# State space scan with C broadcast by DMA and ScalarE, D term on TensorE and its tail on GpSimd; one merged mask in differential attention

## What is computed

```python
def _L2_attn_ref(x, ...):            # differential attention, 32 maps of width 8
    att = einsum('bhtd,bhsd->bhts', q, k) * (1.0 / sqrt(hd))
    att = softmax(where(causal, att, -inf), axis=-1)
    att = att.reshape(B, H, 2, T, T)
    att = att[:, :, 0] - lambda_full * att[:, :, 1]
    out = einsum('bhts,bhsd->bhtd', att, v)
    out = out * rsqrt(mean(out * out) + EPS) * gamma * (1.0 - LAMBDA_INIT)
    return out.reshape(B, T, C) @ w_proj

def _L3_attn_ref(x, ...):            # state space, 512 channels, 16 states
    x_in, z = split(x @ W_in)
    xc = silu(conv4(x_in))                      # 4 taps
    dt, Bm, Cm = split(xc @ W_x, [16, 16, 16])
    delta = softplus(dt @ W_dt + b_dt)
    for t in frames:
        h = h * exp(delta * -exp(A_log)) + (delta * xc) * Bm
        y = sum_over_states(h * Cm)
    y = (y + xc * D) * silu(z)
    hh = x + y @ W_out
    return (hh - mean(hh)) * rsqrt(var(hh) + 1e-5) * gamma + beta
# the tower: h = h + _L2_attn_ref(_layernorm(h), ...) ; later h = h + _L3_attn_ref(_layernorm(h), ...)
```

## Time and profile before

| | us |
|---|---|
| median of 3 runs (lowest to highest) | 4446.45 (4444.82 to 4450.03) |
| the profiled execution | 4441.89, its span 4440.2 |
| differential attention, its loop over utterances | 1494 to 2078 |
| state space, scope | 2740 to 3915 |

### The profile page before, as it was taken

How to read it: one execution, slowest core, us unless ns; L and a number is a source line. 1 busy time by engine, 2 the same in 40 slices (tenths; PEclk the granted TensorE clock), 3 DMA queues, 4 the chain that set the end, 5 groups by cost and what they waited for, 6 DMA issues and landing times. The chain is left out here.

```text
span 4440.2 us, 70612 instructions
## 1 busy us (share of the span) xinstructions
PE 3466.3 (78%) x23831; PEld 2262.3 (51%) x23832; DVE 2241.4 (50%) x4136; ACT 1150.8 (26%) x2267; POOL 1169.3 (26%) x904
## 2 busy tenths in 40 slices
PE   7589954669975999998149961678887788759999
PEld 3367732347753677776139951333333333245777
DVE  0444455224443355554523333478988889941343
ACT  2221110111211122122224420344433444303222
POOL 0112211011211233332530026344444444510121
PEclk9798866778888999998579985789888888869999
DMA  1000002630002000001521112000000000000000
GB/s 43 11 1 0 0 2 43 99 42 0 0 11 83 1 0 0 0 0 33 148 52 47 47 47 56 28 21 25 25 21 21 21 24 25 14 22 0 7 10 11
DMA packets 241137, 115.45 MB, mean 26 GB/s; under 512 B 174305, under 2 KB 225315, under 8 KB 241040
## 3 DMA queue, kind: packets, MB, share of 16 engines
q1 hardware_dynamic: 221136, 98.04, 8.9%
q0 software_dynamic: 18432, 12.40, 1.2%
q10 hardware_dynamic: 1472, 3.85, 0.3%
HBM read 79.03 MB, written 35.02 MB: 26 GB/s over the span
## 5 line engine op out<-in xcount | busy, mean ns | idle before, releaser
L2107 POOL TENSOR_TENSOR ssm_dBx<-ssm_du,ssm_b_wide 128x1488 f32<-128x1488 f32 x128 | 430.1, 3363 | 325.9 <-DVE ssm_state L2364 324.5
L2364 DVE TENSOR_TENSOR_SCAN ssm_state<-ssm_dA,ssm_dBx 128x372 f32<-128x372 f32 x512 | 434.2, 909 | 34.8 <-ACT ssm_dA L2175 19.5
L2254 PE MATMUL ssm_y<-ssm_hC,top_ident 128*128 128x512 f32 (+1 forms) x768 | 430.6, 706 | 9.0 <-DVE ssm_hC L2369 7.5
L2175 ACT ACTIVATE ssm_dA<-ssm_delta,ssm_decay 128x368 f32<-128x368 f32 x512 | 283.1, 568 | 575.0 <-DVE ssm_state L2364 559.5
L2254 PEld LDWEIGHTS ssm_y<-ssm_hC,top_ident 128*128 128x128 f32 x768 | 161.3, 225 | 253.2 <-issue 231.1
L2369 DVE TENSOR_TENSOR ssm_hC<-ssm_state,ssm_c_wide 128x1488 f32<-128x1488 f32 x128 | 218.1, 1704 | 71.4 <-issue 38.2
L657 ACT ACTIVATE dattn_probs<-dattn_scoresT 93x372 f32<-93x372 f32 x256 | 108.1, 472 | 415.4 <-PE dattn_scoresT L570 415.4
L2240 PE MATMUL ssm_c_wide<-ssm_dbc,ssm_pick 48*128 48x372 f32 x256 | 129.9, 592 | 107.0 <-DVE ssm_hC L2369 105.5
L677 DVE TENSOR_REDUCE dattn_negmax<-dattn_scores 93x4 f32<-93x372 f32 x256 | 127.1, 536 | 158.7 <-PE dattn_scores L542 158.7
L1830 POOL DMA_INDIRECT tiles_got<-moe_back,moe_slot x64 | 89.8, 1403 | 376.1 <-DMA moe_back<-tiles_y 356.9
L584 PE MATMUL dattn_outputs<-dattn_v,dattn_probs 93*93 (+1 forms) x2048 | 185.8, 233 | 0.0
(11 more groups left out here) (545 smaller groups left out, 7451.3 us busy)
## 6 DMA issues: line engine op xcount, KB each, us to landing
ssm_b_wide<-b_rows SPq DMA_DIRECT2D x64, 372.0 KB, 3.4
route_stage<-in_L_ffn_W SPq DMA_DIRECT2D x32, 512.0 KB, 4.3
qkv_rows<-rattn_rows SPq DMA_DIRECT2D x32, 288.0 KB, 3.0
rattn_heads<-qkv_rows SPq DMA_DIRECT2D x96, 96.0 KB, 3.4
moe_sent<-top_blank SPq DMA_DIRECT2D x1, 7936.0 KB, 23.7
tiles_x_in<-moe_sent SPq DMA_DIRECT2D x31, 256.0 KB, 2.8
moe_back<-tiles_y SPq DMA_DIRECT2D x31, 256.0 KB, 2.1
tok_frames<-in_frames ACTq DMA_DIRECT2D x8, 376.0 KB, 8.0
```

The lines of the kernel that those rows point to most:

```text
L2107: pool.tensor_tensor(dBx[:, k % 2, :, :], du[:, :, :], b_wide[:, q % BUFS, k % 2, :].unsqueeze(1).broadcast_to([P, CC, GT]), ALU.mult).the ...
L2175: act.activation(by_utterance(dA[:, ring(k, c), 0:GT])[:, :, 1:], by_utterance(delta[:, c, :])[:, :, 1:], ACT.Exp, scale=decay[:, c, k:k + ...
L2254: mm = pe.matmul(ps_y[:, at], ident[:, :], hC[:, k % 2, :, :].rearrange("p c t -> p (c t)")[:, at], start=(k == 0), stop=(k == N - 1))
L2364: dve.tensor_tensor_scan(state[:, k % 2, c, :], dA[:, ring(k, c), 0:GT], dBx[:, k % 2, c, :], 0.0, ALU.mult, ALU.add).then_inc(scanned, 1)
```

## The change

In differential attention the 32 maps are kept as `parts` = 2 halves of 16: `split` and `maxT` get a dimension for the half, both halves use the same 16 selector rows, and the 32 rows of maxima of a half leave room for the mask, so that all causal attentions use the merged mask. The matmuls with `mask_k` go, and `turn_max` makes two transposes. For 16 maps `parts` is 1 and the instructions stay what they were.

In the state space:
- B and C both go to DRAM and come back as broadcast rows (`bc_wide`): two DMAs for each pair of states instead of one. ACT copies C from there to `ps_c`, between the third and the fourth dA of a state, after hC(k-1). `widen` and `pick` are gone.
- The D term is a matmul of PE with `diag(D)` into `ps_y` (`skip`) at k=9, ahead of that state's y. DVE's end of a group is one multiplication of `ps_y` with the gate.
- The normalised rows of the next group are made by ACT at k=1 (scale and bias per partition; a table of biases for all utterances is made once).
- The final norm is four ACT instructions at k=3, with the bias from one more small POOL instruction; gamma, beta and the addition to `hidden` are three POOL instructions at k = 5, 7 and 9.

```diff
@@ attention: constants, turn_max, scores_t, split, max_t
-        self.merged = causal and 2 * maps + T <= P
-        self.maxT = s.sb("maxT", [P, T], BF16)
+        self.parts = maps // HEADS
+        self.sel = s.sb("sel", [P, HEADS, T], BF16)
+        self.split = s.sb("split", [P, self.parts, 2 * HEADS], BF16)
+        self.maxT = s.sb("maxT", [P, self.parts, T], BF16)
+        for part in range(a.parts):
+            mm = pe.transpose(a.ps_g[0:2 * HEADS, 0, :].bitcast(BF16)[:, part * P:part * P + T], a.split[0:T, part, :],
+                              ident16[0:T, 0:T])
+        mm.then_inc(a.max_turned, 1)
-        if masked:
-            for half in range(2):
-                pe.matmul(a.ps_t[0:T, half, 0:GT], ident16[:, 0:T], a.mask_k[:, :, :], start=True, stop=False,
-                          skip_group_check=True)
-                mm = pe.matmul(a.ps_t[0:T, half, j * T:(j + 1) * T], a.sel[:, a.first_map(2 * p + half) + j, :],
-                               a.maxT[:, :], start=False, stop=True, skip_group_check=True)
+                part, row = divmod(a.first_map(2 * p + half) + j, HEADS)
+                mm = pe.matmul(a.ps_t[0:T, half, j * T:(j + 1) * T], a.sel[:, row, :], a.maxT[:, part, :],
+                               start=False, stop=True, skip_group_check=True)
@@ state space, SyncE
                         if q:
                             sync.wait_ge(dbx_ready, N * g + (2 * q + 1))
+                            sync.wait_ge(c_ready, N * g + (2 * q + 1))
+                        for k in range(2):
+                            sync.dma_start(bc_wide[:, q % BUFS, k, :, :].rearrange("p r t -> p (r t)"),
+                                           scratch[bass.ds(g, 1), k, 2 * q:2 * q + 2, :].rearrange("g r t -> (g r t)")
+                                           .partition_broadcast(P)).then_inc(b_loaded[q % BUFS], 16)
@@ state space, GpSimd
+                    pool.wait_ge(rooted2, g + 1)
+                    pool.tensor_tensor(rroot[0:T, 2, :], rroot[0:T, 1, :], ragg[0:T, 0, :], ALU.mult).then_inc(bias_ready, 1)
+                def finish(g, piece):   # gamma, beta, the addition to hidden: three tensor_tensor of 93 x 1024
+                        if started and k == 1:
+                            root(g - 1)
+                        if started and k in (5, 7, 9):
+                            finish(g - 1, (5, 7, 9).index(k))
@@ state space, ScalarE
+                def norm(g, j):         # four activations of 93 x 256, at k == 1
+                def scale(g):           # four activations of 93 x 256, at k == 3
+                            if c == CC - 1:
+                                act.wait_ge(b_loaded[k // 2 % BUFS], 64 * g + 32 * (k // 2 // BUFS + 1))
+                                act.wait_ge(hc_ready, N * g + (k + 4))
+                                act.activation(ps_c[:, 0:GT], bc_wide[:, k // 2 % BUFS, 1, k % 2, :], ACT.Copy).then_inc(c_ready, 1)
@@ state space, TensorE
-                def widen(g, j, k):
-                    pe.matmul(ps_c[:, 0:GT], pick[:, k, :], dbc[:, j, :], start=True, stop=True).then_inc(c_ready, 1)
+                def skip(j):            # at k == 9, between the wait for hC(9) and y(9)
+                    for c in range(CC):
+                        cuts = sorted({c * GT, (c + 1) * GT, *(x for x in (512, 1024) if c * GT < x < (c + 1) * GT)})
+                        for a, z in zip(cuts, cuts[1:]):
+                            pe.matmul(ps_y[:, a:z], diag[:, c, :], xc[:, j, c, a - c * GT:z - c * GT], start=False, stop=False,
+                                      skip_group_check=True)
@@ state space, VectorE
-                            if not last:
-                                norm(g + 1, 1 - j)
-                        if started and k in FINISH_AT:
-                            finish(g - 1, FINISH_AT.index(k))
-                    for c in range(CC):
-                        dve.scalar_tensor_tensor(xc[:, j, c, :], xc[:, j, c, :], cols[:, 2, c:c + 1], ps_y[:, c * GT:(c + 1) * GT],
-                                                 ALU.mult, ALU.add).then_inc(y_taken, 1)
-                    dve.tensor_tensor(xc[:, j, :, :], xc[:, j, :, :], gate[:, j, :, :], ALU.mult).then_inc(yT_ready, 1)
+                    dve.tensor_tensor(flat(xc[:, j, :, :]), ps_y[:, 0:CC * GT], flat(gate[:, j, :, :]), ALU.mult).then_inc(yT_ready, 1)
```

More of the change, by code:

```diff
@@ L387, in __init__ @@
             self.mask_q = s.sb("mask_q", [P, 4, T], BF16)
-            if not self.merged:
-                self.mask_k = s.sb("mask_k", [P, 4, T], BF16)
         self.ps_s = s.ps("scores", [P, 2, 512])
@@ L563, in scores_t @@
             rows = slice(half * P // 2, (half + 1) * P // 2)
-            pe.matmul(a.ps_t[0:T, half, 0:GT], a.k[rows, buf, c, :], a.q[rows, buf, c, v:v + 4, :], start=not masked,
+            pe.matmul(a.ps_t[0:T, half, 0:GT], a.k[rows, buf, c, :], a.q[rows, buf, c, v:v + 4, :], start=True,
                       stop=False, skip_group_check=True)
@@ L682, in split @@
         dve.wait_ge(a.maxed, 2 + (b + 1) * a.units)
-        dve.tensor_copy(a.split[0:T, 0:a.maps], a.negmax[0:T, :]).then_inc(a.half_split, 1)
+        high, low = (a.split[0:T, :, k * HEADS:(k + 1) * HEADS] for k in range(2))
+        negmax = a.negmax[0:T, :].rearrange("p (a m) -> p a m", a=a.parts)
+        dve.tensor_copy(high, negmax).then_inc(a.half_split, 1)
         dve.wait_ge(a.half_split, b + 1)
-        dve.tensor_tensor(a.split[0:T, a.maps:2 * a.maps], a.negmax[0:T, :], a.split[0:T, 0:a.maps],
+        dve.tensor_tensor(low, negmax, high,
                           ALU.subtract).then_inc(a.split_ready, 1)
@@ L691, in max_t @@
         dve.wait_ge(a.scoredT, a.units * (b + 2))
-        dve.tensor_copy(a.maxT[0:2 * a.maps, :], a.ps_g[0:2 * a.maps, 0, :].bitcast(BF16)[:, 0:T]).then_inc(a.maxT_ready, 1)
+        dve.tensor_copy(a.maxT[0:2 * HEADS, :, :], a.ps_g[0:2 * HEADS, 0, :].bitcast(BF16).rearrange("p (a t) -> p a t", t=P)
+                        [:, 0:a.parts, 0:T]).then_inc(a.maxT_ready, 1)
     def behind(b, buf, p):
@@ L2094, in root @@
                     pool.tensor_tensor(rroot[0:T, 1, :], rroot[0:T, 0, :], minus_half[0:T, 0:GU], ALU.pow).then_inc(rooted2, 1)
+                    pool.wait_ge(rooted2, g + 1)
+                    pool.tensor_tensor(rroot[0:T, 2, :], rroot[0:T, 1, :], ragg[0:T, 0, :], ALU.mult).then_inc(bias_ready, 1)
+                def finish(g, piece):
+                    rows = res[0:T, :, :]
+                    if piece == 0:
+                        pool.wait_ge(scaled, GU * g + GU)
+                        pool.tensor_tensor(rows, rows, gamma[0:T, :].unsqueeze(1).broadcast_to([T, GU, D]), ALU.mult
+                                           ).then_inc(tail_step, 1)
+                    elif piece == 1:
+                        pool.wait_ge(tail_step, 2 * g + 1)
+                        pool.tensor_tensor(rows, rows, beta[0:T, :].unsqueeze(1).broadcast_to([T, GU, D]), ALU.add
+                                           ).then_inc(tail_step, 1)
+                    else:
+                        at = bass.ds(GU * g, GU)
+                        pool.wait_ge(tail_step, 2 * g + 2)
+                        pool.tensor_tensor(hidden[0:T, at, :], hidden[0:T, at, :], rows, ALU.add).then_inc(group_done, 1)
                 def group(g, j, last):
+                    started = not (isinstance(g, int) and g == 0)
                     pool.wait_ge(sp_ready, g + 1)
@@ L2178, in group @@
                             ahead(g + 1, 1 - j, k)
+                        if k == 3 and not (isinstance(g, int) and g == 0):
+                            scale(g - 1)
                         if k == 7:
@@ L2285, in _ @@
                 steps_ahead = GroupSteps(dve, step_ahead, 0, 4)
-                steps = GroupSteps(dve, step, 0, 1 + 6 + 4 + 2)
-                def norm(g, j):
-                    n.xn = xns[j]
-                    norm_group_dve(dve, n, g, hidden)
-                norm(0, 0)
+                steps = GroupSteps(dve, step, 0, 1 + 6)
                 for k in range(TAPS):
@@ L2394, in _ @@
                 epilogue(G - 1, 1)
-                for piece in range(len(FINISH_AT)):
-                    finish(G - 1, piece)
 def expert_attention(nc, shared, dram):
```

132 lines of the change are left out of this document (55 added, 77 removed).

## The result

The changed kernel took **4244.21 us** (median of 4 runs, 4233.91 to 4246.77), the kernel before 4446.84 beside it: a ratio of 0.9543, 95% interval [0.9531, 0.9556]. Its profiled execution took 4244.99, with a span of 4243.3; the forecast was 4269 (4235 to 4328). So 203 us came off where 177 were forecast. That is inside the range, but 25 us from its centre and next to the fourth rival (4248), to which the forecast had given 0.12.

What follows compares the result with a forecast made beforehand. PE bounds the differential attention loop, a chain across engines the state space. From the profiled 4441.89 us, 124 (state space) and 53 (attention) come off, giving 4265; the median was forecast at 4269 us, range 4235 to 4328.

Steps and rivals of the forecast that it cites:

- fourth rival: State space group boundary: PE, idle 2 instead of 7 us, stays fast through y(15) and the projection; 4248 us; chance 0.12.
- Attention, -53 (-32 to -67): Differential attention: 128 pairs of mask matmuls leave PE, 56 us; less 2 for added transposes and 1 for the context wait.
- Scan 0 at S + 11.95, with dBx late next: State space: a group's first scan starts 11.95 us after the previous group's last scans start (S), not 16.8, waiting for dBx.
- Projection from S + 11.6, 10.0 long, done at 21.6: Group boundary on PE: output projection starts 5.2 us earlier, 11.6 us after the last scans start (S), and still takes 10.0.
- DVE waits 4.0 for the epilogue's second half; scan 1 at 25.1; first convolution at 37.8.: Group boundary: DVE waits 4.0 us for the projection; times count from the last scans' start; first convolution was at 52.4.
- First convolution to S 82.1, convolutions 7.62 apart.: Rest of a state space period, to the next last scans (S): 84.6 us becomes 82.1 as three widens leave the convolutions.
- second rival: State space: PE's clock stays low through k=1 to 7, adding 231 us; 4500 us, slower than before; chance 0.03.
- Widening: 0.82 each, 2.5 in this stretch.: State space convolutions on PE: three widenings of C at 0.82 us each go, 2.5 us a period.
- The finish steps count for nothing in a period.: State space, k=2 to 7: norm, gamma, beta steps cost DVE 12.4 us a group, hidden where PE and ACT set pace.
- The normalised rows, 5.39 off the chain.: Group boundary: four normalised rows, 5.39 us on DVE, move to ACT, where they cost at most 1.9 us.
- D term hidden on PE at k=9; DMAs, C's copy, GpSimd's tail hidden.: State space: D term's 2.6 to 4 us on PE, the doubled DMAs, ACT's copies and POOL's three steps delay nothing.
- Ends: -6, -20, +2.5, +1.6.: State space scope, us outside the six periods: first group -6, last group -20, start +2.5, end +1.6.

Runs made afterwards that it cites:

- before_warm: The kernel before, with 14 matmuls that compute nothing put on PE ahead of the output projection in each group: 4424.43 us, ratio 0.9959.
- c_by_pe: The changed kernel with C's rows widened by PE again, no copy of C on ACT and no DMA of C: 4313.83 us, ratio 0.9705.
- finish_on_dve: The changed kernel with the final norm's scaling, gamma, beta and the addition into hidden put back on DVE: 4282.87 us, ratio 0.9627 to the kernel before.
- d_on_dve: The changed kernel with the D term put back on DVE and none on PE: 4282.62 us, ratio 0.9641 to the kernel before.
- gate_first: The changed kernel with ACT's Silu of the gate, and its table load, moved ahead of the wait for the last convolution: 4234.22 us, ratio 0.9523.

## Why the prediction was right, and where it was not

The mechanism was right: a chain at the group's end, dBx next to be late, and PE's pace in the convolutions. The size was off. Step by step, against the trace of after unless a run is named.

- **Attention, -53 (-32 to -67).** Came -47 in the profiled execution, -49 as a mean over ten. PE stays full, so the price by distance to what follows (0.45 a pair) was the right kind; 347 ns as a mean of one would have given 89. The clock was lower, 0.95 over the loop for 0.97 before, and 0.66 in its last 28 us for 0.98 at the old loop's end; that this is what is missing is not shown. As the same code differs by 10 us between executions, 4 us are no error of a step that these runs could show. The cover of the context got thin as said: PE waits for it a little in 29 of 32 utterances, 6.8 us in all on its weight loads; 1 was taken, 0 to 7 the bound.
- **Scan 0 at S + 11.95, with dBx late next.** 12.16, and the waits of all 7 such scans end with dBx, 1.1 to 1.5 us each.
- **Projection from S + 11.6, 10.0 long, done at 21.6.** From 10.7, 7.15 long, done at 17.85. **This step failed.** The row of 10.01 was taken over as if it were a property of the matmuls, while the same paragraph removed most of the wait of 7 us ahead of it; before_warm shows the one from the other. It was also the longest of eight (mean 9.04). The earlier start is y(15), 3.70 for 4.68. The clause on the clock, "y(15) and the projection at full clock give 3", had the size (3.9 in after with all that follows) and half the way: the projection ran at full clock, y(15) did not (granted 0.74). So had the rival; its chance, 0.12, was much too low, because the rows at both clocks and the gaps ahead of them were there to be read.
- **DVE waits 4.0 for the epilogue's second half; scan 1 at 25.1; first convolution at 37.8.** 0, 21.4 and 34.8: the same error passed on; 0.7 of it went again, mainly as y(1), 4.89 long, held y(2).
- **First convolution to S 82.1, convolutions 7.62 apart.** 81.3 and 7.42. y between convolutions takes 2.66 with the copy of C gone from PE's row. The second rival (4500) did not come near. The rule of the Trainium skill's page "TensorE: Matmul & The Clock Gate", section "HAM oscillation — how this bites in real kernels", that bursts behind pauses start at half clock, agrees with the projection of the kernel before (granted 0.50 behind 7.0). But y(1) of after was slow behind only 1.28 and the projection of after at full clock behind 1.80, so the pause right ahead doesn't decide alone.
- **Widening: 0.82 each, 2.5 in this stretch.** In c_by_pe 3.7 in the stretch. Its place ahead of hC(0) was in the forecast; that it also stands ahead of y(1) and y(2) at the low clock (2.4) was not named, but is in the 52.4 us that the forecast replaced as a whole.
- **The finish steps count for nothing in a period.** The old trace bears it out, though no run took them off there: the convolutions are 8.43 apart in all of its groups, with no wait on ACT. At the new pace they cost 3.4 a period (finish_on_dve). So the stretch came out near 82.1 only because the same change also moved these steps: without that, C's path would have given less than was counted for it.
- **The normalised rows, 5.39 off the chain.** The 5.39 was a length beside GpSimd; put back in the new surroundings they cost 1.4. What they were worth in the old ones no run shows.
- **D term hidden on PE at k=9; DMAs, C's copy, GpSimd's tail hidden.** Right: the D term's 12 records stand at 3323.83, take 4.2 (2.6 to 4 forecast), and no scan or hC waits for them; all waits of `hC` sum to 5.1 us over the scope, none of them named for the copy or a DMA; GpSimd's three steps take 2.33 to 2.36 (2.3 estimated).
- **Ends: -6, -20, +2.5, +1.6.** The first group -5.1, the start +2.9, the last group and the end together -21.1 where -18.4 was forecast.
- **Sum of the state space, -124.** -149, of which six periods give 126 for 102.
- **Luck.** Split by what was undone, a period's forecast of 17.1 had 4.8 for the D term, 5.4 for the rows, 0 for the finish steps and some 6.9 for C's path; put back one at a time in after they cost 4.3, 1.4, 3.4 and 9.9 (what each was worth in the kernel before can differ). Errors of both signs met, and that the total lies in the range is in part luck.

## What to carry to other kernels

A matmul's duration in a trace holds for the clock that TensorE had there, and in these traces that changed with the waits ahead of it. Where a change removes the wait ahead of a burst of TensorE, price the burst with a row that has no wait ahead of it, and give the difference its own line in the sum. Read the row in every group first: the one taken here was the longest of eight.

A step that is hidden is hidden by something. Once the cover itself is made shorter, price the hidden steps again, and follow them through the engine that empties the buffers, not only along the data; and where a small step is long beside another engine's, look at which of the two starts first before taking its length over.

## What the runs showed of the hardware

- The same 32 matmuls of 256 columns took 7.14 to 7.15 us behind waits of 0.85 to 1.8 (after and seven groups of before_warm) and 8.5 to 10.2 behind waits of 4.0 to 7.0 (before, d_on_dve), with no steady relation inside that span. In the earlier trace rows the first half had a granted clock of 0.50.
- The wait right ahead is not all: y(1) of after took 4.89 at a granted clock of 0.56 behind a wait of 1.28; in the 8.8 us ahead of it PE was busy for 4.2.
- 3.3 us of matmuls that compute nothing, put into the gap of each of 8 groups, made the kernel 19 us faster (0.9959 [0.9945, 0.9974]).
- Four VectorE steps of 93x256 took 1.38 us where GpSimd's product of 3.3 us began behind them, and 5.39 where it began among them. A product of 128x1488 with both inputs in SBUF took 1.96 to 4.8 us beside GpSimd, and 1.71 in the last group, where GpSimd stood still; with one input in PSUM it took 1.71 beside GpSimd too.
- One and the same attention loop differed by up to 10 us in 570 between executions, with stretches of 100 us at 0.93 to 0.98 of the clock at other places each time. A forecast of such a part can't be held to less from one trace.
- Going from Exp to Silu and back costs ScalarE a table load of 1.28 us each way, in rows of their own; gate_first put the first of them and one Silu (1.43) into a wait, and the period fell by 2.75.
